# Causal attention with fp32 queries and keys, one head at each 32 partitions

## The reference, cut to what matters

```python
h = layernorm(x, ln2_g, ln2_b)
q = (h @ q_w).reshape(Bsz, L, 16, 16).transpose(0, 2, 1, 3)
k = (h @ k_w).reshape(Bsz, L, 4, 16).transpose(0, 2, 1, 3)     # v alike
q = q * cos + rot(q) * sin                                     # k alike
sc = jnp.einsum('bhqd,bhkd->bhqk', q, k) / 4.0                 # k, v: 4 query heads share one
p = jax.nn.softmax(sc + causal_mask, -1)                       # fp32
x = jnp.einsum('bhqk,bhkd->bhqd', p, v).reshape(Bsz, L, D) @ o_w + x
```

## Time and profile before

| | us |
|---|---|
| median of three runs | 4013.91 |
| the profiled execution's own time | 4019.58 |
| its span | 4017.7 |
| TensorE busy over the span | 3371.3 (84%) |
| VectorE busy | 2484.0 (62%) |
| ScalarE busy | 1680.3 (42%) |
| GpSimd busy | 1168.8 (29%) |

### The profile page before, as it was taken

One profiled execution on the slowest core, in us unless ns is written; L12 is line 12 of the kernel. 1 busy time (PEld: TensorE's weight loads), 2 busy tenths in 40 slices (PEclk: granted clock), 3 DMA queues, 4 the chain that ended last, 5 costly groups with the idle time before them and its releaser, 6 DMA issues. The chain is left out here.

```text
span 4017.7 us, 46219 instructions
## 1 busy us (share of the span) xinstructions
PE 3371.3 (84%) x16242; PEld 1650.9 (41%) x16242; DVE 2484.0 (62%) x5354; ACT 1680.3 (42%) x2670; POOL 1168.8 (29%) x1015
## 2 busy tenths in 40 slices
PE   6899989897668988999988979994997478878799
PEld 2344334342323323333323235552555255555466
DVE  2999999999727768767768613335662244556212
ACT  4556556554213555554555622211121344434332
POOL 2767776667432000221000000000222333311110
PEclk9999999999968999999999989996998688888899
DMA  2222222212141122022121010003122256453100
GB/s 76 74 66 71 70 67 69 67 65 73 48 71 39 25 30 36 26 49 46 21 30 24 10 50 11 11 6 101 62 91 95 80 135 133 119 118 68 35 21 21
DMA packets 187783, 232.16 MB, mean 58 GB/s; under 512 B 56763, under 2 KB 134031, under 8 KB 184195
## 3 DMA queue, kind: packets, MB, share of 16 engines
q1 hardware_dynamic: 184482, 220.84, 21.7%
q0 software_dynamic: 3072, 8.39, 0.7%
HBM read 183.26 MB, written 45.89 MB: 57 GB/s over the span
## 5 line engine op out<-in xcount | busy, mean ns | idle before, releaser
L1287 ACT ACTIVATE g_pT<-PS 128x1024 f32<-128x1024 f32 (+3 forms) x640 | 552.4, 894 | 466.9 <-PE PS L1593 276.7
L379 POOL TENSOR_TENSOR WB<-m_dtx,WB 128x1024 f32<-128x1024 f32 x256 | 600.9, 2351 | 294.3 <-DVE WB L523 262.9
L1433 DVE TENSOR_REDUCE g_mxp<-PS 128x1 f32<-128x512 f32 x768 | 491.8, 686 | 91.4 <-PE PS L1574 87.4
L411 ACT ACTIVATE PS<-m_dt,m_A 128x512 f32<-128x512 f32 x512 | 353.2, 691 | 433.0 <-DVE WB L514 432.4
L1574 PE MATMUL PS<-g_KT,WB 96*128 96x512 bf16 (+3 forms) x1280 | 423.3, 363 | 120.0 <-DVE g_mxp L1433 57.2
L608 PE MATMUL PS<-WB,ident 128*128 128x512 f32 x1024 | 503.0, 614 | 0.0
L514 DVE TENSOR_TENSOR_SCAN WB<-PS,m_state,WB 128x512 f32<-128x512 f32 x384 | 472.2, 1275 | 14.9 <-ACT PS L411 14.7
L1593 PE MATMUL PS<-WB,g_KT 99*128 99x512 bf16 (+3 forms) x1280 | 359.1, 353 | 1.2 <-ACT g_pT L1287 0.6
L1574 PEld LDWEIGHTS PS<-g_KT,WB 96*128 96x128 bf16 x1280 | 110.4, 98 | 503.8 <-DVE g_mxp L1433 260.4
L523 DVE TENSOR_TENSOR WB<-WB,PS 128x1024 f32<-128x1024 f32 x256 | 308.8, 1206 | 5.8 <-PE PS L594 2.4
L1426 DVE CUSTOM_DVE_ANT_0 PS<-PS,g_mq 128x384 f32<-128x384 f32 (+3 forms) x512 | 246.5, 507 | 98.6 <-PE PS L1574 92.0
(11 more groups left out here) (311 smaller groups left out, 5227.8 us busy)
## 6 DMA issues: line engine op xcount, KB each, us to landing
WB<-b_rows SPq DMA_DIRECT2D x256, 256.0 KB, 3.1
WB<-in_L_ffn_w SPq DMA_DIRECT2D x18, 1024.0 KB, 7.5
WB<-g_dq SPq DMA_DIRECT2D x96, 128.0 KB, 4.1
g_rden<-g_dn SPq DMA_DIRECT2D x128, 64.0 KB, 2.0
w_dv<-WA SPq DMA_DIRECT2D x16, 512.0 KB, 4.5
w_V<-w_dv SPq DMA_DIRECT2D x16, 512.0 KB, 10.7
w_rden<-w_dn SPq DMA_DIRECT2D x128, 64.0 KB, 2.1
g_dq<-g_parts SPq DMA_DIRECT2D x16, 384.0 KB, 2.5
```

The costliest lines, as they stand in the source:

```text
L379: pool.tensor_tensor(hh[:, g % RING, :, :], dtx[:, MB * h:MB * h + MB, :], Bs[:, g % BRING, :].unsqueeze(1) .broadcast_to([P, MB, CH]), AL ...
L411: act.activation(PS[:, 2 + b, :], dt[:, c % 2, m, :], ACT.Exp, scale=Aneg[:, n, m:m + 1]).then_inc(dA_ready, 1)
L1287: act.activation(pT[:, n % 2, 2 * pair:2 * pair + 2, 0:width], PS[:, 2 * pair:2 * pair + 2, at:at + width], ACT.Exp, scale=DH ** -0.5).the ...
L1433: dve.tensor_reduce(mxp[:, q % 6, i % QB, hh:hh + per, at], scores[:, :, 0:width], AX.X, ALU.max)\
```

## The change

The causal attention gets a stage of its own, with a planner of its own (`CausalPlan`); the band attention keeps the old one. Queries and keys stay fp32. Head hh of a block lies at partitions 32 hh to 32 hh + 16, so that the four heads lie in four groups of 32 partitions; the keys are loaded four times, once to each group. Row 17 of a group has the maxima on the query side and ones on the key side (`KQ` = 17). The parts and their acts are gone, a build has 9 DMAs, and `pool.memset(KT, 1.0)` sets 8192 columns at the start.

A max act is now two heads: 640 acts in place of 1280, each of two matmuls with 16 rows, in two different groups of partitions, to two banks. Max acts and uses share a ring of three banks (4, 5, 7): each matmul of a max act and each use takes the next bank of the ring, and waits until the bank's last content has been read. A max act claims both of its banks before its first matmul. In most windows the order is: max of heads 2 and 3, turn of heads 0 and 1, max of heads 0 and 1, turn of heads 2 and 3, pv of the window before. A diagonal window's masks come after both turned matmuls of a pair, on the full array. The operations of the VectorE, ScalarE and the pv act stay as they were, apart from the bank they read.

```diff
+MAX_BANKS = (4, 5, 7)
+KQ = DH + 1
+        lead, build_lead, step, rate = 5, 6, 0.6, 1.06
+        told, multiplied, projected, gap = 4.5, 9, 10.5, 0.7
+        for n in range(len(self.windows)):
+            acts += [(n, "turn", n, 0), (n + 0.25, "turn", n, 1), (n + 1.45, "pv", n)]
+        for m, ((q, w), n) in enumerate(zip(maxima, when)):
+            early, late = (0.6, 0.65) if m and when[m - 1] == n else (-0.01, 0.24)
+            acts += [(n + early, "max", 2 * m, q, 2, w), (n + late, "max", 2 * m + 1, q, 0, w)]
...
+        self.ring, i = {}, 0
+        for what, *x in self.order:
+            if what == "max":
+                self.ring["max", x[0]] = i
+                i += 2
+            elif what == "use":
+                self.ring[tuple(x)] = i
+                i += 1
...
+        def rows_of(hh, n):
+            return slice(32 * hh, 32 * hh + n)
+        def bank(i):
+            return PS[:, MAX_BANKS[i % 3], :]
...  # gpsimd
+                pool.memset(o_w, 0.0).then_inc(zeroed, 1)
+                pool.memset(KT, 1.0).then_inc(ones_set, 1)
...  # vector
+                    if what == "max":
+                        for e in range(2):
+                            r = ring["max", m] + e
+                            dve.wait_ge(mx, 2 * m + e + 1)
+                            scores = bank(r)[:, 0:width]
+                            if m_width:
+                                ins = dve.tensor_tensor_reduce(...)
+                            else:
+                                ins = dve.tensor_reduce(to, scores, AX.X, ALU.max)
+                            ins.then_inc(bank_free[r % 3], 1)
...  # tensor
+                def claim(i):
+                    if i >= 3:
+                        pe.wait_ge(bank_free[i % 3], i // 3)
+                    if what == "max":
+                        for e in range(2):
+                            claim(ring["max", m] + e)
+                        for e in range(2):
+                            rows = rows_of(hh + e, DH)
+                            pe.matmul(bank(ring["max", m] + e)[:, 0:width],
+                                      QT[rows, u % QRING, g, P * (i % QB):P * (i % QB) + P],
+                                      KT[rows, region(s, k0 // CH), g, 0:width],
+                                      start=True, stop=True).then_inc(mx, 1)
+                    elif what == "turn":
+                        if n:
+                            pe.wait_ge(ex, 2 * n + pair - 1)
+                        for hh in (2 * pair, 2 * pair + 1):
+                            rows = rows_of(hh, KQ)
+                            mm = pe.matmul(PS[:, hh, at:at + width],
+                                           KT[rows, region(s, j // QB), g,
+                                              P * (j % QB):P * (j % QB) + P],
+                                           QT[rows, chunk(q) % QRING, g, at:at + width],
+                                           start=True, stop=not m_width)
+                        if m_width:
+                            for hh in (2 * pair, 2 * pair + 1):
+                                mm = pe.matmul(PS[:, hh, at:at + m_width], k.identb[:, :],
+                                               mask_k[:, m_at:m_at + m_width],
+                                               start=False, stop=True)
+                    elif what == "use":
+                        kind, i = x[0], ring[tuple(x)]
+                        claim(i)
```

More of the change, by code:

```diff
@@ L9 @@
+import math
 from contextlib import ExitStack
@@ L1660, in _, with __init__ @@
                         mm.then_inc(w_full, 1)
-def stage_causal_attention(k):
-    stage_attention(k, True)
+MAX_BANKS = (4, 5, 7)
+KQ = DH + 1
+class CausalPlan:
+    def __init__(self):
+        scores, turned = causal_windows()
+        lead, build_lead, step, rate = 5, 6, 0.6, 1.06
+        told, multiplied, projected, gap = 4.5, 9, 10.5, 0.7
+        span, apart = 12, (6, 18)
+        self.windows, self.first = [], []
+        for q in range(NQ):
+            self.first.append(len(self.windows))
+            self.windows += [(q, w) for w in turned[block_of(q)[1]]]
+        self.first.append(len(self.windows))
+        acts = []
+        for n in range(len(self.windows)):
+            acts += [(n, "turn", n, 0), (n + 0.25, "turn", n, 1), (n + 1.45, "pv", n)]
+        maxima = [(q, w) for q in range(NQ) for w in scores[block_of(q)[1]]]
+        at, when, ended, began = float("inf"), [], {}, {}
+        for q, w in reversed(maxima):
+            at = min(at, self.first[q] - lead)
+            ended.setdefault(q, at)
+            at -= 1 / rate
+            began[q] = math.floor(at) - 0.02
+            when.append(math.floor(at))
+        when.reverse()
+        self.last_max = {}
+        for m, ((q, w), n) in enumerate(zip(maxima, when)):
+            early, late = (0.6, 0.65) if m and when[m - 1] == n else (-0.01, 0.24)
+            acts += [(n + early, "max", 2 * m, q, 2, w), (n + late, "max", 2 * m + 1, q, 0, w)]
+            self.last_max[q] = 2 * m + 1
+        uses = []
+        for q in range(NQ):
+            closed = self.first[q + 1] + 0.45
+            uses.append((ended[q] + 1.0, "rows", q))
+            uses += [(closed + projected + 1.2 * gap * r, "out", q, r) for r in range(2)]
+            acts += [(ended[q] + 0.1, "parts", q), (closed + 0.2, "den", q),
+                     (closed + told / 2, "den_in", q), (closed + told, "inv", q),
+                     (closed + told + 0.1, "inv_out", q),
+                     (closed + (told + multiplied) / 2 - 0.2, "inv_in", q),
+                     (closed + multiplied, "mul", q)]
+        need = []
+        for u in range(NS * NJ):
+            need.append(began[2 * u])
+            acts.append((need[u] - build_lead, "build", u))
+        end = float("inf")
+        prepared = []
+        for b in reversed(range(B)):
+            for c in reversed(range(NJ)):
+                end = min(need[2 * NJ * b + c] - build_lead - 5 * step - 1, end - apart[b])
+                prepared.append((b, c, end - span))
+        for b, c, begin in reversed(prepared):
+            for i, kind in enumerate(("t0", "t1", "q0", "r0", "q1", "r1", "k", "v")):
+                uses.append((begin + i * span / 8, kind, b, c))
+        taken, placed = [], []
+        for kind, way in (("rows", 1), ("out", 1), (None, -1)):
+            chosen = [x for x in uses if x[1] == kind or kind is None and
+                      x[1] not in ("rows", "out")]
+            limit = None
+            for p, *key in sorted(chosen, key=lambda x: way * x[0]):
+                p = p if limit is None else way * max(way * p, way * limit)
+                for y in sorted(taken, key=lambda y: way * y):
+                    if abs(y - p) < gap - 1e-9:
+                        p = y + way * gap
+                limit = p
+                taken.append(p)
+                placed.append((p, *key))
+        self.use, self.item, self.source, ready = {}, {}, [], {}
+        for i, (at, *key) in enumerate(sorted(placed)):
+            self.use[tuple(key)] = i
+            acts.append((at, "use", *key))
+            kind = key[0]
+            if kind == "out" and key[2] and key[1] % 2 and block_of(key[1])[0] % 2:
+                acts.append((at + 1.0, "stats", key[1]))
+            if kind == "rows":
+                acts.append((at + 2 * step, "rows_in", *key[1:]))
+            if kind == "t0":
+                acts.append((at - 4 * step, "hn", *key[1:]))
+            if kind in ("r0", "r1", "k"):
+                it = len(self.item)
+                self.item[("q" + kind[1] if kind[0] == "r" else kind, *key[1:])] = it
+                self.source.append(tuple(key))
+                acts += [(at + step, "sum", it), (at + step * 3, "store", it, *key)]
+                ready[key[1], key[2]] = at + step * 3
+            if kind == "v":
+                acts.append((at + 2 * step, "store_v", *key[1:]))
+        for u, p in enumerate(need):
+            assert ready[u // (2 * NJ), u % NJ] < p - build_lead
+        self.order = [a[1:] for a in sorted(acts, key=lambda a: a[0])]
+        self.ring, i = {}, 0
[6 more added lines that the diff above has]
+                i += 1
```

429 lines of the change are left out of this document (added).

## The result

| | before | after |
|---|---|---|
| median, us | 4016.84 (4 runs, 4012.73 to 4019.99) | 4927.29 (4 runs, 4897.26 to 4941.43) |
| profiled execution's own time / span | 4019.58 / 4017.7 | 4941.43 / 4939.6 |
| mean granted TensorE clock, whole span | 0.93 | 0.784 |
| first max act to end of the last pv act | 1157.0 | 2111.0 |
| mean granted clock in that stage | 0.966 | 0.601 |

The ratio is 1.226, 95% interval 1.220 to 1.232. The forecast was 4255 (4130 to 4480). The stage grew by 954 us; the first max act came 21.7 us earlier (1150.6 for 1172.3), and what follows the stage took 10 us less (1678.0 for 1688.3). 954 - 21.7 - 10.3 = 922 us, the whole difference of the two profiled executions.

What follows compares the result with a forecast made beforehand. Neither TensorE nor VectorE was full; the max act was taken as the TensorE's gate. Intervals of 1318 us plus 60, 13 and 22 made 1413 for 1157; 4019.6 + 256 - 15 = 4260, 6 less for the median: 4255 us (4130 to 4480).

Steps and rivals of the forecast that it cites:

- the early phase: 39 max acts before the first turn, run alone with the clock at 0.64: 22 us more.
- The clock rival: TensorE stays at 1.2 GHz because it waits in every interval: 5060 us; chance 0.09 together with no overlap.
- The chain of the max acts: Each max act waits for the VectorE's first-head read: 1.90 us per unmasked act, 2.01 with a pv.
- The masked intervals: Intervals of masked max acts: 134 without a pv at 196 us, 64 with one at 122 us.
- The four side by side: Two max heads and two turned heads on four row groups cost the TensorE what one matmul would, 0.855 us.
- the rival with the turn behind the max: The turn starts only after the max's last pass; intervals with pv grow by 0.855 us: 4450 us, chance 0.18.
- The rival of no overlap: Row groups do not run side by side, a window takes 7.9 us: 5240 us; chance 0.09 together with half clock.
- The last rival: Not slower: the chain does not bind, only the TensorE's own work is left: 4015 us, chance 0.10.
- Uses in the ring: 126 intervals between max acts hold uses that take ring banks: 339 us for 104 of them, 49 for 22.
- The intervals without a use: 513 intervals between max acts with no use, full and masked, with or without pv: together 930 us.
- the terms outside the intervals: Last 20 windows without max acts 60 us, 62 output additions 13 us, early half clock 22 us.
- The start: Three banks for uses before the first max act bring it 15 us earlier (between 0 and 25).

Runs made afterwards that it cites:

- Experiments 3: The kernel before with its bf16 max matmuls cut from 96 rows to the first 16; 4404.19 us, one run.
- experiment 8: The changed kernel, exact, with each of a max act's two banks claimed just before its own matmul; 4785.4 us, ratio 1.192 to the kernel before.
- experiment 1: The changed kernel with all score matmuls over 32 rows, exponential's scale 1e-6, output not the reference's; 4350.31 us, ratio 1.078 to the kernel before.
- experiment 2: The changed kernel with only the turned matmuls over 32 rows, max acts at 16, result unchanged; 4475.67 us, ratio 1.110 to the kernel before.
- experiment 5: The changed kernel, exact, with two full bf16 matmuls (128 rows, 512 columns) added per window; 4639.09 us, ratio 1.155 to the kernel before.

## Why the prediction was wrong, by its own steps

**The failed step** is one assumption, that outside of the early phase the clock stays as it was. It stands in the sum (22 us for the early phase and nothing for the rest), and the argument that held it up was in the rivals: "where the TensorE waited more, the clock was 0.64; against: it will still be busy in two thirds of each window". That read the row with the lowest clock as a matter of waiting. The runs showed the rows in its place: a stage clock of 0.60, where padding to 32 rows gives 0.94 and 594 us back. Experiments 3 and 8 are 95% and 99% busy and have 0.73 and 0.64. I knew that the rows of the score matmuls fell from 96 to 16 and used it for the length of a pass only, where it indeed changes nothing.

**The size of that term.** The price of a stretch at half clock fits: the forecast turned 1318 us of intervals into 2120, a factor of 1.61. After, 80% of 2111 us, 1684, ran at 1.2 GHz, an excess of 1684 x (1 - 1/1.61) = 638 us; in experiment 1, with 12% of 1517, 70 us. The difference, 568, stands beside the 594 that the widening gave back. Only the share was wrong: I had put "a tenth more of the stage" as the bound. The clock rival (0.09 for it and for missing overlap together) came nearest, 5060 for 4927, and its mechanism is the one that happened, though not for its reason: a TensorE that never waits has the low clock too (experiment 8).

**The chain of the max acts** was right: in full intervals near full clock 1.97 us for 1.90 and, with a pv, 2.10 for 2.01; after, where most of them ran at half clock, 2.91 and 3.92. The masked intervals were too short in the sum: 222 us without a pv for 196, and 146 with one for 122 (experiment 1).

**The four side by side** was right; the rival with the turn behind the max (4450) is out, since they start within 0.02 us. The rival of no overlap is out too. (The last rival's sum, 1161 for 1157, gives 4018 us and not 4015; nothing rests on it.)

**Uses in the ring** were undersized: 445 us in the 126 intervals that hold one, for 388. The intervals without a use were 80 us over. Together 137 us, of which the terms outside the intervals gave back 33 (62 us for the 95 of last windows, output additions and early clock). That is the whole 104 between the forecast's 256 and the 360 us that experiment 1 added to the stage: the sizes at nearly full clock were 104 us short, and the clock term 594. Part of the 104 is clock too: experiment 1 has by the estimate above 70 us of half clock, where the forecast had 22.

**The start** gained 21.7 us for 15, within its bounds. After the last pv all was as before, within 10 us.

**What should have shown it.** Of the listed signs those of the chain came true (four matmuls within 0.1 us, VectorE at 836, first act earlier), and so did the one named as making the forecast wrong, a granted clock below 0.9 in the middle. Two signs came true only at nearly full clock: acts 1.9 us apart and a window of 3.9 (1.97 and 4.07 in experiment 1; 2.91 and 6.83 after), and the lower TensorE busy share (0.84 in experiment 1; after it is 0.90 as before, because half clock stretches the matmuls over the gaps).

## What to carry to other kernels

A matmul that uses few rows of the array costs the same time by itself, but in this stage a stream of them lost the full clock even when the TensorE was busy 99% of the time: before cutting a contraction from 96 rows to 16, look at what else keeps the array full, and read the granted clock of the stretch before any other view of the profile after. If few rows can't be avoided, padding the row groups to 32 with zeros (4927 to 4476 us here, with half of the score matmuls padded), or a full matmul thrown in, can be worth more than it costs. And test a change that joins several ideas part by part: its ring of three banks alone was worth 2.8%.

## What the runs showed of the hardware that was not expected

- Rows of zeros raised the granted clock: in experiment 2 rows 17 to 31 of the turned matmuls' Q hold nothing but zeros (K has ones there), and the stage's clock rose from 0.60 to 0.85. Whether the chip counts rows addressed, or something that goes with them, was not taken apart further, nor was any number of rows between 32 and 96 tried.
- Four fp32 matmuls of 16 and 17 rows in four row groups start within 0.02 us of each other, although two of them stand behind another semaphore wait. Over 32 rows (experiment 1) four cost 0.98 us for one's 0.855.
- Useless work made a kernel faster: 640 added matmuls, 288 us less (experiment 5).
